# Graph layer and expert layer in one kernel: gathers issued a block further ahead, expert weights loaded in place of their low parts, and the last group's gates in banks of their own

## The reference

```python
def _L0_gnn_ref(x, edge_index, W1, b1, W2, b2):          # x is 2500 x 512, 80000 edges
    agg = jax.ops.segment_sum(x[src], dst, num_segments=N_NODES)
    h = jax.nn.relu(((1.0 + eps) * x + agg) @ W1 + b1)
    return h @ W2 + b2

def _L0_ffn_ref(x, Wg, W1, b1, W2, b2):                  # 8 experts, 512 -> 256 -> 512
    gate = jax.nn.softmax(xt @ Wg, axis=-1)
    topv, topi = jax.lax.top_k(gate, 2)
    scores = ...                                         # the two shares of each row, summing to 1
    for e in range(E):
        h = jax.nn.gelu(xt @ W1[e] + b1[e], approximate=False)
        out = out + (h @ W2[e] + b2[e]) * scores[:, e:e + 1]

x = x + _L0_gnn_ref(_layernorm(x, axis=-1), edge_index, ...)
x = x + _L0_ffn_ref(_layernorm(x, axis=-1)[None], ...)[0]
```

## Time and profile before

| | |
|---|---|
| median of 3 runs | 702.55 us |
| the profiled execution, its own time | 706.18 us |
| its span in the trace | 704.5 us |
| PE busy | 602.3 us, 85% |
| DVE busy | 449.5 us, 64% |
| ACT busy | 308.3 us, 44% |
| POOL busy | 271.3 us, 39% |

### The profile page before, as it was taken

How to read it: one execution, slowest core, us unless ns; L and a number is a source line. 1 busy time by engine, 2 the same in 40 slices (tenths; PEclk the granted TensorE clock), 3 DMA queues, 4 the chain that set the end, 5 groups by cost and what they waited for, 6 DMA issues and landing times.

```text
span 704.5 us, 10590 instructions
## 1 busy us (share of the span) xinstructions
PE 602.3 (85%) x3822; PEld 434.0 (62%) x3823; DVE 449.5 (64%) x765; ACT 308.3 (44%) x565; POOL 271.3 (39%) x223
## 2 busy tenths in 40 slices
PE   0798999999999999999999999733998999989810
PEld 0345666666566766676666566633897888879700
DVE  2855988987897699769872222759565444444441
ACT  1554554332422241233223103361786676666762
POOL 4074222040610070007000510362577768767663
PEclk9999999999999999999999999955999999999965
DMA  9344000100211111201120213772789979888895
GB/s 242 124 121 145 1 1 1 60 1 1 60 45 45 46 45 45 69 21 46 45 87 4 88 44 105 235 224 78 226 164 189 188 172 189 181 179 168 181 181 71
DMA packets 38955, 72.51 MB, mean 103 GB/s; under 512 B 8597, under 2 KB 12749, under 8 KB 38387
## 3 DMA queue, kind: packets, MB, share of 16 engines
q0 software_dynamic: 13280, 29.88, 21.6%
q1 hardware_dynamic: 23073, 37.02, 17.6%
q10 hardware_dynamic: 2550, 4.93, 2.6%
HBM read 46.74 MB, written 26.10 MB: 103 GB/s over the span
## 4 chain that ended last, share of the span: by engine, by line
PE 58%; POOL 11%; DMA 11%; DVE 7%; ACT 6%; issue 5%; ACTq 2%; POOLq 0%; DVEq 0%; SPq 0%
PE psum L1243 24%; PE psum L1226 11%; PE psum L1168 9%; POOL out_x L562 7%; PE psum L1280 7%; DMA out_x<-y,target_i 6%; DMA xg<-xt_d,token_i 4%; POOL xg L555 3%; PE psum L1305 2%; PE psum L1158 1%; PE psum L1298 1%; ACT y L770 1%; ACTq L587 1%; ACT h L644 1%; PE psum L1228 1%
## 5 line engine op out<-in xcount | busy, mean ns | idle before, releaser
L928 DVE TENSOR_TENSOR hot_key<-iota_key,key_w 128x1600 f16<-128x1600 f16 x125 | 136.0, 1088 | 42.3 <-PE psum L1228 41.0
L622 ACT ACTIVATE counts<-psum 128x400 bf16<-128x400 f32 x125 | 62.6, 505 | 183.0 <-PE psum L1228 183.0
L562 POOL DMA_INDIRECT out_x<-y,target_i x54 | 88.8, 1644 | 44.8 <-ACT y L770 16.8
L1226 PE MATMUL psum<-hot_key,hot_lo 128*128 128x200 f16 x1000 | 103.7, 249 | 2.5 <-DVE hot_lo L928 2.1
L1226 PEld LDWEIGHTS psum<-hot_key,hot_lo 128*128 128x128 f16 x1000 | 86.6, 98 | 29.6 <-issue 7.9
L928 DVE TENSOR_TENSOR hot_lo<-iota_lo,lo_w 128x1024 f16<-128x1024 f16 x125 | 104.5, 836 | 0.0
L1243 PE MATMUL psum<-counts,z_hi 125*128 125x500 bf16 x400 | 101.6, 375 | 1.5 <-ACT h L644 1.4
L1243 PE MATMUL psum<-counts,z_lo 125*128 125x500 bf16 x400 | 100.7, 374 | 0.0
L526 POOL TENSOR_TENSOR h_lo<-h,h_hi 128x500 fp32r<-128x500 f32 x16 | 24.6, 1567 | 190.4 <-ACT h_hi L651 190.4
L1127 DVE TENSOR_TENSOR he_lo<-he,he_hi 128x256 fp32r<-128x256 f32 x54 | 23.0, 425 | 84.9 <-ACT he L761 72.2
L1168 PE MATMUL psum<-W_sb,xT 128*125 128x512 f32 x160 | 72.7, 597 | 0.1
(11 more groups left out here) (214 smaller groups left out, 1078.2 us busy)
## 6 DMA issues: line engine op xcount, KB each, us to landing
w_raw<-in_L_ffn_W SPq DMA_DIRECT2D x16, 512.0 KB, 6.4
b_now<-in_L_ffn_b SPq DMA_DIRECT2D x27, 256.0 KB
x_res<-in_x SPq DMA_DIRECT2D x20, 224.0 KB
out_x<-x SPq DMA_DIRECT2D x20, 224.0 KB
xt_d<-xt SPq DMA_DIRECT2D x20, 224.0 KB
x_in<-in_x ACTq DMA_DIRECT2D x2, 1120.0 KB
x_in<-in_x SPq DMA_DIRECT2D x2, 1120.0 KB
W_sb<-in_L_gnn_W ACTq DMA_DIRECT2D x1, 1024.0 KB, 6.9
```

What stands on the lines that cost most here:

```text
L562: pool.indirect_dma_start(out=out[:, :], in_=y[:, k % 2, i], in_offset=None, out_offset=bass.IndirectOffsetOnAxis(ap=target_i[:, 2 * k + i ...
L622: act.activation(counts[:, it % 2, :, place:place + W], psum[:, WIN + w % 2, 0:MW].rearrange("p (w h) -> p h w", w=W), ACT.Copy).then_inc( ...
L928: ins = dve.tensor_tensor(hot[:, w % RING].rearrange("p s (n two) -> p s n two", two=2), iota[:].rearrange("p (o n two) -> p o n two", o=1 ...
L1226: mm(psum[:, WIN + w % 2, a * MH:(a + 1) * MH], hot_lo[:, w % RING, k], hot_key[:, w % RING, k], start=(k == 0), stop=False)
```

## The change

Four things are changed.

1. `gather(k + 4)` stands where `gather(k + 3)` stood, and four blocks are gathered ahead of the loop instead of three. The number of buffers stays 3.
2. The buffers `w_raw` are gone: each expert's weights are loaded where its low part will stand, and DVE subtracts in place. All eight have a place, so no load waits for a split. SP loads expert 3 between the stores of the last group, 4 behind them, and 5 to 7 right after it has told the others that the rows have landed. POOL subtracts nothing any more. DVE does expert 0's W1 ahead of the last `gate_take`, four more splits at the places where it did those of 3 and 4, and one in each of the blocks k = 0 to 10 (11 in all, where 6 stood in k = 1 to 6). ACT rounds experts 5 to 7 ahead of `take_block(0)` instead of in blocks 0 to 5.
3. The gates of the last group use the banks AGG + q, one for each tile, and wait for no `gate_taken`. DVE takes the logits of q = 0 between the residuals of q = 2 and 3.
4. PE turns block 0 after 24 of the 40 steps of the score product instead of after all 40.

```diff
--- before.py
+++ after.py
 PAD = 512
 SCALE = 32768.0
 XB = 3
-RAWS = 3
+AHEAD = 5
...
@@ -181,17 +182,29 @@
 
         ffn = ExitStack()
         sb = allocator(ffn)
-        w_raw = sb("w_raw", [128, RAWS, 2, KC * H], F32)
-        w1_hi, w1_lo, w2_hi, w2_lo = [], [], [], []
+        w1_raw, w2_raw, w1_hi, w1_lo, w2_hi, w2_lo = [], [], [], [], [], []
         for e in range(NE):
-            if e == NE - 1:
-                spread = ExitStack()
-                at_row = allocator(spread)("at_row", [P, 2 * T, 128], F16)
-                at_tile = allocator(spread)("at_tile", [P, 2 * T, NT], F16)
-                spread.close()
-            for name, tensors, shape in (("w1_hi", w1_hi, [128, KC, H]), ("w1_lo", w1_lo, [128, KC, H]),
-                                         ("w2_hi", w2_hi, [128, HC, D]), ("w2_lo", w2_lo, [128, HC, D])):
-                tensors.append(sb(f"{name}_{e}", shape, F32R))
+            for name, raws, hi, lo, shape in (("w1", w1_raw, w1_hi, w1_lo, [128, KC, H]), ("w2", w2_raw, w2_hi, w2_lo, [128, HC, D])):
+                hi.append(sb(f"{name}_hi_{e}", shape, F32R))
+                in_place = ExitStack()
+                raws.append(allocator(in_place)(f"{name}_raw_{e}", shape, F32))
+                in_place.close()
+                lo.append(sb(f"{name}_lo_{e}", shape, F32R))
+
+        work = ExitStack()
...
             def load_expert(e):
-                if e >= RAWS:
-                    sp.wait_ge(S["w_hi_ready"], e - RAWS + 1)
-                    sp.wait_ge(S["w_lo_ready"], e - RAWS + 1)
-                sp.dma_start(w_raw[:, e % RAWS, 0].rearrange("p (k h) -> p k h", k=KC),
-                             eW1[e].rearrange("(k p) h -> p k h", p=128)).then_inc(ew_in[e % RAWS], 16)
-                sp.dma_start(w_raw[:, e % RAWS, 1].rearrange("p (k h) -> p k h", k=HC),
-                             eW2[e].rearrange("(k p) h -> p k h", p=128)).then_inc(ew_in[e % RAWS], 16)
+                sp.dma_start(w1_raw[e][:], eW1[e].rearrange("(k p) h -> p k h", p=128)).then_inc(ew_in[e], 16)
+                sp.dma_start(w2_raw[e][:], eW2[e].rearrange("(k p) h -> p k h", p=128)).then_inc(ew_in[e], 16)
...
             sp.wait_ge(S["agg_done"], G)
-            for e in range(RAWS):
+            for e in range(3):
                 load_expert(e)
             store(G - 2, 3)
             load_residual(G - 1, 3)
-            for q in range(4):
+            store(G - 1, 0)
+            load_expert(3)
+            for q in (1, 2, 3):
                 store(G - 1, q)
-            for e in range(RAWS, 2 * RAWS):
-                load_expert(e)
+            load_expert(4)
             for q in range(4):
                 sp.wait_ge(x2_out[q], 64 * G)
             sp.wait_ge(S["spare_out"], 16)
             sp.sem_inc(S["x2_landed"], 1)
+            for e in range(AHEAD, NE):
+                load_expert(e)
             sp.wait_ge(S["gate_done"], T)
             sp.dma_start(eb1_col[:], eb1.rearrange("e (k p) -> p (e k)", p=128), allow_slow_non_contiguous=True).then_inc(S["eb_in"], 16)
...
@@ -447,8 +445,6 @@
             sp.wait_ge(S["spread_done"], 1)
             load_bias(0)
             load_bias(1)
-            load_expert(6)
-            load_expert(7)
             for k in range(NB):
                 if k >= 1 and k + 1 < NB:
                     load_bias(k + 1)
...
 
-            def split_low(e):
-                pool.wait_ge(S["w_hi_ready"], e + 1)
-                pool.tensor_tensor(w1_lo[e][:], w_raw[:, e % RAWS, 0].rearrange("p (k h) -> p k h", k=KC), w1_hi[e][:].bitcast(F32), ALU.subtract)
-                pool.tensor_tensor(w2_lo[e][:], w_raw[:, e % RAWS, 1].rearrange("p (k h) -> p k h", k=HC), w2_hi[e][:].bitcast(F32), ALU.subtract)\
-                    .then_inc(S["w_lo_ready"], 1)
-
             pool.wait_ge(S["small_in"], 48)
...
             pool.wait_ge(S["x2_landed"], 1)
             pool.wait_ge(S["tokens_ready"], 1)
-            for k in range(XB):
+            for k in range(XB + 1):
                 gather(k)
             for k in range(NB):
                 if k == 0:
                     pool.wait_ge(S["targets_ready"], 1)
-                if k + XB <= NB:
-                    gather(k + XB)
+                if k + XB + 1 <= NB:
+                    gather(k + XB + 1)
...
-                bank = WIN + q % 2 if g == G - 1 else SM if q == 2 else SM + 1
+                bank = AGG + q if g == G - 1 else SM if q == 2 else SM + 1
...
             def split_high_up(e):
-                act.wait_ge(ew_in[e % RAWS], 32 * (e // RAWS + 1))
-                act.activation(w1_hi[e][:], w_raw[:, e % RAWS, 0].rearrange("p (k h) -> p k h", k=KC), ACT.Copy).then_inc(S["w1_hi_ready"], 1)
+                act.wait_ge(ew_in[e], 32)
+                act.activation(w1_hi[e][:], w1_raw[e][:], ACT.Copy).then_inc(S["w1_hi_ready"], 1)
 
             def split_high_down(e):
-                act.activation(w2_hi[e][:], w_raw[:, e % RAWS, 1].rearrange("p (k h) -> p k h", k=HC), ACT.Copy).then_inc(S["w_hi_ready"], 1)
+                act.activation(w2_hi[e][:], w2_raw[e][:], ACT.Copy).then_inc(S["w_hi_ready"], 1)
...
             std2(G - 1, 3)
-            split_high_down(1)
             gate_rows(G - 1, 2)
             gate_rows(G - 1, 3)
+            split_high_down(1)
             split_high(2)
...
             act.activation(token_part[:, :, 0], at_tile[:], ACT.Copy, scale=iota_p[:]).then_inc(S["parts_ready"], 1)
+            for e in range(AHEAD, NE):
+                split_high(e)
...
                 if k + 2 <= NB:
                     take_block(k + 2)
-                if k < 6:
-                    (split_high_up, split_high_down)[k % 2](5 + k // 2)
...
             gate_take(G - 2, 3)
-            for q in range(1, 4):
+            for q in (1, 2):
                 residual(G - 1, q)
                 residual_end(G - 1, q)
-            for q in range(4):
-                gate_take(G - 1, q)
-
+            gate_take(G - 1, 0)
+            residual(G - 1, 3)
+            residual_end(G - 1, 3)
+            gate_take(G - 1, 1)
+            gate_take(G - 1, 2)
 
             def split_low_up(e):
                 dve.wait_ge(S["w1_hi_ready"], e + 1)
-                dve.tensor_tensor(w1_lo[e][:], w_raw[:, e % RAWS, 0].rearrange("p (k h) -> p k h", k=KC), w1_hi[e][:].bitcast(F32), ALU.subtract)
+                dve.tensor_tensor(w1_lo[e][:], w1_raw[e][:], w1_hi[e][:].bitcast(F32), ALU.subtract)
 
             def split_low_down(e):
                 dve.wait_ge(S["w_hi_ready"], e + 1)
-                if e == RAWS:
-                    dve.wait_ge(S["w_lo_ready"], RAWS)
-                dve.tensor_tensor(w2_lo[e][:], w_raw[:, e % RAWS, 1].rearrange("p (k h) -> p k h", k=HC), w2_hi[e][:].bitcast(F32), ALU.subtract)\
-                   .then_inc(S["w_lo_ready"], 1)
-
+                dve.tensor_tensor(w2_lo[e][:], w2_raw[e][:], w2_hi[e][:].bitcast(F32), ALU.subtract).then_inc(S["w_lo_ready"], 1)
+
+            split_low_up(0)
+            gate_take(G - 1, 3)
             dve.wait_ge(S["topi_ready"], T)
             step(dve.tensor_copy(topf[:], topi[:, :, 0:2].rearrange("p n c -> p c n")))
             experts = iota_e[:].rearrange("p (o e) -> p o e", o=1).broadcast_to([P, T, NE])
@@ -1074,7 +1062,7 @@
             step(dve.tensor_scalar(expert_f[:], expert_f[:], float(NE - 1), None, ALU.min))
             dve.tensor_copy(expert_i[:], expert_f[:])
             dve.tensor_copy(end_i[:], block_end[0:1]).then_inc(S["slots_known"], 1)
-            split_low_up(3)
+            split_low_down(0)
             dve.wait_ge(S["spread_done"], 1)
...
-            split_low_up(4)
-            split_low_down(4)
+            split_low_up(1)
+            split_low_down(1)
+            split_low_up(2)
             turned_low(0)
             dve.wait_ge(S["score_spread"], 1)
...
                 turned_low(k + 1)
-                if 1 <= k < 7:
-                    (split_low_down, split_low_up)[k % 2](5 + (k - 1) // 2)
+                if k < 11:
+                    (split_low_down, split_low_up)[k % 2](2 + (k + 1) // 2)
                 dve.wait_ge(b2_in[k % 2], 16 * (k // 2 + 1))
                 if k >= 2:
                     dve.wait_ge(y_out[k % 2], 32 * (k // 2))
...
             def gate_bank(g, q):
-                return WIN + q % 2 if g == G - 1 else SM if q == 2 else SM + 1
+                return AGG + q if g == G - 1 else SM if q == 2 else SM + 1
 
             def gate_turn(g, q):
                 n = 4 * g + q
                 pe.wait_ge(S["xt_ready"], n + 1)
-                if g == G - 1:
-                    if q >= 2:
-                        pe.wait_ge(S["gate_taken"], n - 1)
-                elif q == 0:
+                if g < G - 1 and q == 0:
                     pe.wait_ge(S["x2_ready"], n + 2)
-                elif q == 1:
+                elif g < G - 1 and q == 1:
                     pe.wait_ge(S["gate_taken"], n)
...
             for n in range(2 * T):
+                if n == 24:
```

(2 more changed lines are left out.)

35 lines of the change are left out of this document (17 added, 18 removed).

## The result

The changed kernel takes **691.4 us** (median of 4 runs, 690.27 to 692.61) against 702.73 us for the kernel before in the same session (4 runs, 701.82 to 704.24): ratio 0.9837, interval 0.9812 to 0.9861, 11.3 us less. The forecast was 689.5 us, range 684.5 to 695.5.

A forecast was written before the change was run, and what follows sets the result against it. The prediction took POOL to bound the block loop, with a chain of waits through the routing ahead of it. Its terms summed to -13.0 us from the profiled 706.18; less 3.6 us distance to the median, 689.5 us, range 684.5 to 695.5.

The forecast's parts named there:

- The likeliest case: Whole kernel: all terms come as summed, 689.5 us, itself 686 to 692.5; chance 55%.
- the second: Block loop: waits for `y` return as waits for landing or PE, so 696.9 us; chance 13%.
- the sixth: Before block 0: loads of experts 5 to 7 crawl and hold it, making the kernel slower, 704.5 us; chance 5%.
- the fourth: Before the loop: gates or routing give half, 3 us less gain, 692.5 us; chance 9%.
- the third: Block loop: each of five more DVE splits holds POOL's issue for 1.22 us, 694.9 us; chance 8%.
- gates: Last group's gates: with own banks, one transpose and one gate move into PE's idle time, -1.6 us.
- POOL's splits: stretch: Routing: without POOL's splits beside them, DVE's `chosen` and `topf` shorten by 2.0 and 0.8 us.
- POOL's splits: tables: Routing: the ranking product no longer waits for POOL's tables, kept back by its weight split; 2.1 us.
- turn(0): Ahead of block 0: PE starts turning it as soon as `x_now` is ready, -0.6 us.
- block 0's split ahead of `y`: Block 0: a DVE split of 1.22 us delays the `y` POOL waits for, +0.8 us.
- loop: gathers and held adds: Block loop: earlier gathers remove waits for `y`, -3.6 us; more DVE splits hold POOL's adds, +0.7 us.
- the loop's end: Behind block 23's first add: the last add comes 15.6 instead of 19.4 us later, -3.8 us.

The follow-up runs named there:

- the last four runs: On one chip: changed kernel 692.54 us, with DVE's splits behind `y` 691.09, with three `y` buffers 691.04, with both edits 688.96; kernel before 704.79.
- the gathers alone: Kernel before with only its gathers moved one block ahead; 697.54 us against 704.42, ratio 0.9898.
- gates undone: Changed kernel with the last group's gate banks, waits and DVE order as before, the split still ahead of the last gate; 695.55 us, ratio 0.9826.
- POOL's splits back: Changed kernel with POOL doing five splits of experts 0 to 2 behind its tables instead of DVE; 695.92 us, ratio 0.9868.
- turn undone: Changed kernel with block 0 turned behind all 40 steps of the score product again; 694.40 us, ratio 0.9817.
- both gather runs: Kernel before with gathers a block ahead, 697.54 us, and changed kernel with gathers in their old place, 697.65 us.
- the split behind `y`: Changed kernel with DVE's splits of blocks 0 to 10 behind `y` instead of ahead, run on two chips; 690.17 and 691.09 us.
- after: First profiled execution of the changed kernel, nothing further changed; 690.27 us.
- after again: Changed kernel profiled a second time, nothing changed; 693.31 us.
- after timed: Changed kernel unchanged, timed and profiled beside three variants on one chip; 692.54 us, ratio 0.9817.
- `y3`: Changed kernel with three buffers for `y` instead of two; 691.04 us, ratio 0.9797.

## Why the prediction was right, point by point

**Sign, size and cause hold.** 11.3 us came where 13.0 were forecast (12.3 on the chip of the last four runs). The likeliest case was the one that happened; of the rivals, the second (the loop gives nothing) fell with the gathers alone at -6.9, the sixth (late loads) with 6.10 us of idle time left, the fourth with the ranking product 7.7 us earlier, the third because of DVE's eleven splits in the loop only three held an add for over 0.1 us, in each of three traces of the changed kernel. DVE's split ahead of the last gate was covered as forecast: it ended at 462.37, PE's last gate at 462.29. The size is less sure than it looks: the same stages of the same kernel differ between traces by 2 us in the routing (rank 28.0 and 30.1) and by 3 in the loop, so a total within 2 us of the forecast doesn't confirm each term. The first add "near 499.8" does not follow from the terms either: 505.73 - 1.6 - 4.9 - 0.6 + 0.8 is 499.4.

| term | forecast | shown | by |
|---|---|---|---|
| gates | -1.6 | -2.4 | gates undone |
| POOL's splits: stretch | -2.8 | -3.0 | POOL's splits back |
| POOL's splits: tables | -2.1 | -2.0 | the same |
| loads | 0 | 0 | ACT's rows |
| turn(0) | -0.6 | -0.3 | turn undone |
| block 0's split ahead of `y` | +0.8 | +1.6 | first up matmul to first add, 8.5 to 10.1 |
| loop: gathers and held adds | -2.9 | -3 to -5 | both gather runs |
| the loop's end | -3.8 | -2.2 to -2.7 | all traces with early gathers |

- *Gates*: the mechanism was right and the size off. I put 0.62 and "some 1.0" for the transpose and the gate that move into the idle time, while the earlier trace rows had the gate at 3.38 / 2 = 1.69: the low clock's length, at which it was to be removed. The transpose takes 1.07 there.
- *turn(0)*: I counted what stands in front of `turned_low(0)`, and left out that the turn itself would be longer at the place where PE's granted clock was 0.57.
- *Split ahead of y*: half of it. Undoing the gathers left +0.8, exactly as forecast; with early gathers 0.2 to 1.6 more appears (9.45 to 10.85 us in seven traces, against 9.26) between gelu, the turn of block 1 and its high part; with the split behind `y` it is 8.5 to 9.0. I did not find what this is. Nor did the sum have a term for what lies between the ranking product and `x_now` of block 0: 20.95 us instead of 20.55, and 20.2 to 20.9 in the other traces with the new order.
- *Held adds*: the mechanism is in the earlier trace rows and in the rows of after: the add at 529.57 began 0.18 us into a DVE split and took 2.53, that at 516.73 began 0.53 into one and took 2.16. Both end 1.5 us behind the split's end (530.61 and 517.42), so the issue goes on only when the split is through. But the prediction looked at splits alone, and `he_lo` does the same. DVE's and POOL's timeline of after:

```profile
516.20 1.22 DVE L991 TENSOR_TENSOR w_lo<-w_raw,w_hi 128x1024 fp32r<-128x1024 f32 x1
...
529.39 1.22 DVE L991 TENSOR_TENSOR w_lo<-w_raw,w_hi 128x1024 fp32r<-128x1024 f32 x1
...
611.59 0.43 DVE L1115 TENSOR_TENSOR he_lo<-he,he_hi 128x256 fp32r<-128x256 f32 x1 [0.31 <-issue]
611.68 1.83 POOL L549 DMA_INDIRECT out_x<-y,target_i  x1 [0.30 <-issue]
```

  Of the six adds over 1.75 us in after, three began inside a split and three inside a `he_lo`; of the five before, one and four. So the count of long adds (4 to 6 against 3 to 5) doesn't size the term. By splits alone the adds of the loop lost 0.9 to 1.8 us in three traces of the changed kernel and 0.8 to 1.0 in two of the one before. The difference, -0.1 to +1.0, holds the forecast's +0.7 without showing it.
- *The loop*: "the nine for SP unchanged" was wrong. Eight remain in every trace with early gathers where splits and buffers are as in the change, 10.7 to 13.1 us in all; the three traces with late gathers have 12.4 (eight), 14.2 and 16.7 (nine each). The kernel before, run again, had eight as well, so the ninth is not the gathers' alone, and part of the 16.7 was spread of that execution. The waits for `y` are clearer. Less the usual gaps they were 3.6, 3.6 and 2.6 us with late gathers and nothing in the seven with early ones, as forecast; the rest of the loop's gain is in the waits for landing and was not separated.
- *The end*: the step that failed is "from such a start to the next add let go by its landing passed 5.7 us". In the loop's end `y` of block 25 began 7.7 us after the second add of block 23 (661.42), DVE at 669.15:

```profile
661.62 1.29 DVE L1124 TENSOR_TENSOR y<-psum,b_now 128x512 f32<-128x512 f32 x2 [2.25 <-issue]
669.15 1.29 DVE L1124 TENSOR_TENSOR y<-psum,b_now 128x512 f32<-128x512 f32 x2 [2.09 <-issue]
```

In the seven traces it was 7.0 to 7.7 us. Two us more on that landing make 17.6 of the forecast's 15.6; 17.2 was measured, with 5.3 instead of 5.9 for the last empty block. The chain (buffer, landing, `y`, scaling, add) was right, as the third buffer shows; the size of its landing was taken from the loop's first blocks.

The terms shown are -7.4 for the routing, -0.3 and +1.6 up to the first add, -3 to -5 in the loop and -2.2 to -2.7 at its end, together -11.3 to -13.8; the medians give 11.3 and 12.3. That the forecast carried the profiled execution's 3.6 us over to the median was harmless here, but the loop of that trace held 3 us that another trace of the same kernel did not have.

## What to carry to other kernels

Before sizing a stall, look at whether a neighbour engine's instruction ends where the slow one ends: two engines that finish together are held together, and moving the work to the engine that is idle can be worth more than its own time. When a wait of a queue goes away, follow the next shared thing (here a buffer freed only by a landing, then the order of landings) with durations taken from that very place, not from the middle of the loop. A stall's removal on PE should be priced at both granted clocks, since the rows behind idle time are the slow ones.

## What the runs showed of the hardware

- The same 8-step gate took 0.94 us at a granted clock of 1 and 1.69 us at half; block 0's eight transposes 1.05 and up to 1.97 us.
- One execution differs from the next by where the clock falls. Ahead of the transposes of the last group's first tile PE stood idle for 1.69 us, in the changed kernel's second and third traces (after again, after timed) alike:

```profile
445.10 1.09 PE L1283 MATMUL psum<-ident,xt 125*128 125x125 f32 x4 [1.69 <-DVE xt L938]
```

```profile
444.85 0.65 PE L1283 MATMUL psum<-ident,xt 125*128 125x125 f32 x4 [1.69 <-DVE xt L938]
```

  In the first the granted clock over the next 4 us was 0.57 on average, and so it was in `y3`; in the second and in the first trace of the changed kernel it was 1.00. The ranking product came 2.1 us later in the two with the low clock (rank 30.1 against 28.0 and 28.1), and the other traces with the changed kernel's routing whole had 28.0 to 28.4.
- POOL's issue of an indirect transfer that begins inside a DVE split waits for the split's end: adds end 1.5 us behind it, and the gathers of after at 484.42 and 486.34 (1.62 and 1.97 us instead of 1.0) 0.8 us behind it (the splits ended at 485.22 and 487.48). Over all fourteen traces, of the adds that began at least 0.25 us ahead of the end of a DVE instruction, 35 began inside a split (1.76 to 2.65 us long, ending 1.46 to 1.50 behind it) and 28 inside a `he_lo` (1.73 to 1.86, ending 1.46 to 1.51 behind it). Both have two inputs in SBUF. The 230 that began inside `xT_lo` or `y`, which read one input from PSUM and last 0.68 us, took 1.64 at most.
- The kernel before had medians of 702.7, 706.3, 704.4 and 704.8 us in four sessions, with single runs up to 710.7. Versions that were not run side by side can't be compared within 1 to 2 us; the ratios above each go by the kernel before on the same chip.
